# A Swin block on one core: the output projection as three float16 products of an output split on POOL, and a new order at the end of each step

## Chip, cores and metric

The kernel runs on 1 core of one Trainium2 chip. The metric is device time in microseconds (us) of one execution, and versions are compared by the median of several runs.

## What is computed

The input is x, 32 images of 96 channels by 56 by 56 pixels, float32. The reference is one Swin transformer block with shifted windows:

```python
f = roll(ln(x over channels) * g1 + b1, (-3, -3))
win = windows of 7 x 7 tokens                   # 64 windows per image
q, k, v = split(win @ w_qkv + b_qkv)            # 12 heads of 8
attn = softmax(q @ k.T * 8 ** -0.5 + mask)      # mask: shifted regions
out = (attn @ v) @ w_proj + b_proj              # the projection
f = x + roll(unwindow(out), (3, 3))
y = f + gelu(ln(f) @ w_fc1 + b_fc1) @ w_fc2 + b_fc2
```

## The kernel before

**Tiling.** An image is cut into 8 bands of 7 rows; one band is 8 windows, 392 tokens (TOK). There are 256 bands. The program is a software pipeline: one step per band, and in step t each stage works on band t plus a fixed offset. A band is loaded at offset LOAD = 9, reordered into windows on POOL at ORDER = 7, transposed to tokens at TURN = 6, normalised there and transposed back at BACK = 5, multiplied into queries and keys at QK = 4, into values at VALUES = 2; its scores are made and their maximum is taken at SCORE = 2; the shifted scores and their exponentials come at PROB = 0; the weighting with the values, its division, the transposes of the output and the projection at WEIGH = -1. The second layer norm of a finished band rides along with the first of a later one (8 bands apart, AFTER), then the hidden layer follows at offsets -5 and -4, its contraction at -6 and -5, the result at -7 and -6. Even and odd steps differ: the hidden layer of two bands (`expand`, `expand_rest`, Gelu) is done in odd steps, and its contraction (`contract`, L637) in even steps, so work repeats in pairs of steps.

**Order.** Each engine has its own program, written out by hand in a function `step(t)`; nothing reorders it. Engines meet through semaphores that count up. The orders that matter here:

- TensorE (L662). Odd step: three parts of shifted scores (L512), values (L473), scores (L494) and weighting (L530), then `turn` (L555), `expand`, `expand_rest`, `max_transpose` (L597), `out_transposes` (L608), `back` (L570), `queries_keys` (L438), `project` (L618). Even step: scores, weighting, shifted scores, values and so on, `turn`, `out_transposes`, `back`, `max_transpose`, `queries_keys`, `project`, `contract` (L652, L658). The first shifted scores of a step wait for n_low, the low half of the normalised tokens (xfl).
- ScalarE (L772). It takes the exponentials (L719), copies values (L713), writes the high float16 halves xfh (`back_high`, L731) and nat (`queries_keys_high`, L739), copies the transposed output to oT (`out_by_channel`, L753), copies the row of maxima (L745), and does the Gelu in odd steps (L762) and `scaled` in even ones (L770). The Gelu and the exponential each need a table load (ACT_TABLE_LOAD). In odd steps the Gelus come ahead of `out_by_channel`.
- VectorE (L923). The step begins with `residual` (L905) of the step before, which adds the projection in PSUM and the bias to x. In odd steps there follow `back_low` (xfl, L891) and `queries_keys_low` (L898) of the step before, `result` (L920, three additions of two SBUF tensors each) and `maxima` (L856) in turn, then `divide` (L863, L865), the last maxima, `by_token` (L872), `stats` (L880, L885), and `back_low` of this step.
- POOL (L414). Even steps begin with two `split_hidden` (L389 a copy to float16, L392 the subtraction that gives the low half). Every step then has `normalise` (L399, L402, L406, L411) and `order_x` (L378, L381, L382). `normalise` waits in L402 for n_made, that is for `back`; `back` of the next step waits for its result.
- SyncE issues all DMAs: images in and out, and nat by way of DRAM into the stacked operands kst, qbd, qst and kbd.

**Products.** Queries and keys, values, the hidden layer and its contraction are each computed as three float16 products of operands split into a high and a low half (high x high, high x low, low x high). The projection is one float32 product, with oT and wp. In the trace a float32 product has two records.

**Waits that matter.** `back` in an odd step waits for the first Gelu, because it writes the PSUM banks (B) that the Gelu reads:

```python
if odd(t):
    wait(pe, gelu_done, t.step(HIDDEN[0]).count(1, 1)) if has(t.step(HIDDEN[0])) else None
```

## Time and profile before

| what | value |
|---|---|
| median of 3 runs | 2875.02 us (2874.71 to 2877.26) |
| the profiled execution's own time | 2881.17 us |
| its span | 2879.4 us |
| TensorE busy (matmul) | 2719.4 us, 94% |
| VectorE busy | 2398.4 us, 83% |
| ScalarE busy | 2128.1 us, 74% |
| POOL busy | 1847.1 us, 64% |
| DMA | 358.88 MB, mean 125 GB/s |
| mean granted TensorE clock | 0.994 |

How to read it: the span is the time between the first and the last instruction of one profiled execution; durations in the rows below come from that execution. In the rows PE is the matmuls of TensorE and PEld its weight loads, DVE is VectorE, ACT is ScalarE, POOL is GpSimd. L12 is line 12 of the kernel. A matmul's duration reaches to the end of its pipeline, so that matmuls one behind the other overlap in the rows: the distance of two starts is what one costs.

### The profile page before, as it was taken

The numbers are of one execution on the slowest core, as the hardware profiler recorded it, in microseconds if no ns is written. First come the engines' busy times: TensorE is split into PE (matmuls) and PEld (weight loads), VectorE is DVE, ScalarE is ACT, GpSimd is POOL, SyncE is SP. The second block draws the span as 40 slices with busy tenths as digits, with TensorE's granted clock in tenths as the row PEclk, the third lists the DMA queues.
The fourth block names the chain that finished last, engine by engine and source line by source line (L and its number), as shares of the span: only waits on it lengthen the run. The fifth ranks groups of instructions, "written<-read, shape, count | busy, mean of one in ns | idle before, by whom it ended". The sixth has DMA issues, their size and how long they took to land.

```text
span 2879.4 us, 138054 instructions
## 1 busy us (share of the span) xinstructions
PE 2719.4 (94%) x55491; PEld 2243.8 (78%) x55491; DVE 2398.4 (83%) x6634; ACT 2128.1 (74%) x3464; POOL 1847.1 (64%) x2344
## 2 busy tenths in 40 slices
PE   4899999999999999999999999999999999999997
PEld 2787787878878878788788888788777877878875
DVE  7888888888888888888888888888888888888884
ACT  2677777777777777777777777777777777777774
POOL 3466666666666666666666666666666666666665
PEclk9999999999999999999999999999999999999998
DMA  2545545545545544454554554554545455455441
GB/s 73 135 123 132 130 125 129 131 127 131 130 127 132 129 126 127 128 134 126 129 132 124 130 134 124 130 131 125 129 124 131 125 131 133 123 130 134 123 117 29
DMA packets 414852, 358.88 MB, mean 125 GB/s; under 512 B 63646, under 2 KB 414176, under 8 KB 414204
## 3 DMA queue, kind: packets, MB, share of 16 engines
q1 hardware_dynamic: 414220, 350.04, 47.1%
q8 instruction: 447, 7.32, 1.1%
q14 instruction: 185, 1.52, 0.2%
HBM read 193.29 MB, written 154.14 MB: 121 GB/s over the span
## 4 chain that ended last, share of the span: by engine, by line
PE 77%; DVE 8%; ACT 8%; issue 6%; POOL 1%; SPq 0%; DMA 0%; POOLq 0%; DVEq 0%
PE psum L530 18%; PE psum L512 11%; PE psum L438 9%; PE psum L494 8%; PE psum L570 7%; PE psum L555 6%; PE psum L448 5%; DVE xfl L891 4%; ACT probs L719 4%; ACT xfh L731 4%; PE psum L608 3%; PE psum L618 3%; PE psum L456 3%; PE psum L473 2%; PE psum L597 1%
## 5 line engine op out<-in xcount | busy, mean ns | idle before, releaser
L719 ACT ACTIVATE probs<-psum 113x784 f32<-113x784 f32 x768 | 633.2, 824 | 348.6 <-PE psum L512 345.5
L856 DVE TENSOR_REDUCE nmax<-psum 113x16 f32<-113x784 f32 x768 | 743.4, 968 | 69.9 <-PE psum L494 69.8
L530 PE MATMUL psum<-vbd,probs 128*49 128x18 f32 x24576 | 643.8, 197 | 11.6 <-issue 11.4
L530 PEld LDWEIGHTS psum<-vbd,probs 128*49 128x49 f32 x24576 | 633.0, 126 | 15.2 <-issue 14.8
L399 POOL TENSOR_SCALAR ve<-mv 112x7 f32<-112x7 f32 (+1 forms) x264 | 65.9, 250 | 890.6 <-PE psum L570 649.6
L512 PE MATMUL psum<-qbd,kst 128*49 128x196 f16 x6144 | 404.9, 250 | 81.6 <-DVE xfl L891 70.7
L494 PE MATMUL psum<-kbd,qst 128*49 128x196 f16 x6144 | 403.1, 250 | 7.4 <-DVE nmax L856 4.9
L406 POOL TENSOR_TENSOR rs<-ve,half 112x7 f32<-112x7 f32 (+1 forms) x264 | 394.4, 1494 | 0.0
L411 POOL TENSOR_TENSOR xn<-xn,rs 112x672 f32<-112x672 f32 (+1 forms) x264 | 343.0, 1299 | 73.9 <-POOL rs L406 73.9
L891 DVE TENSOR_TENSOR xfl<-psum,xfh 96x784 f16<-96x784 f32 (+1 forms) x264 | 252.9, 958 | 160.7 <-ACT xfh L731 159.5
L880 DVE BATCH_NORM_STATS2 st<-tok 112x6 f32<-112x96 f32 x1824 | 318.3, 246 | 59.2 <-ACT tok L726 45.0
L392 POOL TENSOR_TENSOR hidl<-hid,hidh 128x588 f16<-128x588 f32 x256 | 334.1, 1305 | 46.2 <-POOL hidh L389 46.2
L512 PEld LDWEIGHTS psum<-qbd,kst 128*49 128x49 f16 x6144 | 243.9, 103 | 135.2 <-issue 95.8
L402 POOL TENSOR_TENSOR xn<-tok,mv 112x672 f32<-112x672 f32 (+1 forms) x264 | 343.4, 1301 | 0.5 <-POOL ve L399 0.5
L494 PEld LDWEIGHTS psum<-kbd,qst 128*49 128x49 f16 x6144 | 261.9, 103 | 93.0 <-issue 76.8
L739 ACT ACTIVATE nat<-psum 96x784 f16<-96x784 f32 x256 | 210.0, 820 | 127.8 <-PE psum L438 127.8
L713 ACT ACTIVATE vbd<-psum 49x384 f32<-49x384 f32 x512 | 261.0, 510 | 7.2 <-PE psum L473 1.0
L570 PE MATMUL psum<-ident,xn 112*96 112x112 f32 x1951 | 236.7, 263 | 25.3 <-POOL xn L411 24.2
L920 DVE TENSOR_TENSOR yr<-ys,xf 96x343 f32<-96x343 f32 (+2 forms) x768 | 243.0, 368 | 15.2 <-ACT ys L770 15.2
L898 DVE SCALAR_TENSOR_TENSOR nat<-psum,nat 96x784 f16<-96x784 f32 x256 | 245.8, 960 | 0.0
L731 ACT ACTIVATE xfh<-psum 96x784 f16<-96x784 f32 (+1 forms) x264 | 212.7, 806 | 27.2 <-PE psum L570 26.9
L570 PEld LDWEIGHTS psum<-ident,xn 112*96 112x96 f32 x1951 | 184.3, 127 | 52.2 <-POOL xn L411 25.3
(102 smaller groups left out, 6069.1 us busy)
## 6 DMA issues: line engine op xcount, KB each, us to landing
stack_pages<-nat SPq DMA_DIRECT2D x256, 294.0 KB, 3.0
kst<-stack_pages SPq DMA_DIRECT2D x256, 220.5 KB
qbd<-stack_pages SPq DMA_DIRECT2D x1024, 55.1 KB
stack_pages<-nat SPq DMA_DIRECT2D x256, 147.0 KB, 2.1
xr<-in_x_dram SPq DMA_DIRECT2D x224, 147.0 KB, 2.7
out_dram<-yr SPq DMA_DIRECT2D x224, 147.0 KB, 2.1
qst<-stack_pages SPq DMA_DIRECT2D x256, 73.5 KB
kbd<-stack_pages SPq DMA_DIRECT2D x1024, 18.4 KB
```

Of the source, the lines that this page charges most:

```text
L392: nc.gpsimd.tensor_tensor(hidl[:, n, :, :], hid[:, n, :, :], hidh[:, n, :, :], ALU.subtract).then_inc(hid_low, 1)
L402: nc.gpsimd.tensor_tensor(xn[:, n, 0:groups, :], tok[:, n, 0:groups, :], mv[:, n, 0:groups, 0:1].to_broadcast(wide_by_token), ALU.subtract ...
L406: nc.gpsimd.tensor_tensor(rs[:, n, 0:groups], ve[:, n, 0:groups], half[0:SPAN, 0:groups], ALU.pow).then_inc(root_done, 1)
L411: nc.gpsimd.tensor_tensor(xn[:, n, 0:groups, :], xn[:, n, 0:groups, :], rs[:, n, 0:groups].rearrange("t (g a) -> t g a", a=1).to_broadcast ...
L494: last = nc.tensor.matmul(psum[W1 * w:W1 * w + L, A + p // 2, p % 2 * CH:(p % 2 + 1) * CH], qst[:, masked_slot(b), u, toks], kbd[:, b.c % ...
L512: last = nc.tensor.matmul(wide_bank()[W1 * w:W1 * w + L, LEFT + p // 2 * 4 * SPAN + p % 2 * CH:LEFT + p // 2 * 4 * SPAN + (p % 2 + 1) * CH ...
L530: last = nc.tensor.matmul(dst[:, :, h, :], probs[:, b.c % 2, h // 4, p, h % 4 * L:(h % 4 + 1) * L], vbd[:, b.c % 4, p * NH + h, :, :], sta ...
L570: last = nc.tensor.transpose(wide_bank()[0:C, LEFT + at * SPAN:LEFT + (at + 1) * SPAN], xn[:, b.c % 2, g, :], ident[0:SPAN, 0:SPAN])
L719: nc.scalar.activation(probs[0:PR, b.c % 2, u, :, :].rearrange("j (g q) k -> j g (q k)", g=2), wide_bank()[0:PR, LEFT:LEFT + 8 * SPAN].rea ...
L731: nc.scalar.activation(parts_of(xfh, b), by_channel(b), ACT.Copy).then_inc(n_high, 1)
L856: nc.vector.tensor_reduce(dst, psum[0:PR, A:A + 2, 0:2 * CH].rearrange("i g (q h j) -> i g q h j", q=2, j=L), axis=AX.X, op=ALU.max, negat ...
L891: nc.vector.tensor_tensor(parts_of(xfl, b), by_channel(b), parts_of(xfh, b), ALU.subtract).then_inc(n_low, 1)
```

## The change

The projection becomes three float16 products like the others: weights split once into wph and wpl (`split_wp`, scaled by GAIN = 64), the output split in each step on POOL into oTh and oTl (`split_out`, new, ahead of `normalise` and behind `split_hidden`). The bias b_proj becomes a row of the weights against a row of ones in oTh, and `residual` scales by 1/GAIN in place of adding the bias. `out_by_channel` waits for the split of the band before. `project` waits for the split's low half. In odd steps `out_transposes` moves to behind `turn`, and `out_by_channel` to ahead of the Gelus. In even steps `project` moves behind `contract`, and `back_high` (xfh) comes ahead of `queries_keys_high` (nat). The diff (declarations shortened):

```diff
@@ -117,8 +117,8 @@
         wh, wl = sb("wh", [FULL, 3 * C], F16), sb("wl", [FULL, 3 * C], F16)
         w1h, w1l = sb("w1h", [FULL, HID], F16), sb("w1l", [FULL, HID], F16)
         wp, w2 = sb("wp", [FULL, C]), sb("w2", [FULL, 3, C])
-        vec = sb("vec", [C, 6])
-        G1, B1, BP, G2, B2, BF = range(6)
+        vec = sb("vec", [C, 5])
+        G1, B1, G2, B2, BF = range(5)
 
         xr = sb("xr", [C, 4, WS, SIDE])
         xf = sb("xf", [C, 8, 2, TOK])
@@ -137,7 +137,9 @@
         probs = sb("probs", [FULL, 2, QUADS, PAIRS, CH])
         rsum = sb("rsum", [PR, 2, 2 * NH])
         on = sb("on", [PR, 2, 2, C])
-        oT = sb("oT", [FULL, TOK])
+        oT = sb("oT", [C, TOK])
+        oTh, oTl = sb("oTh", [FULL, TOK], F16), sb("oTl", [FULL, TOK], F16)
+        wph, wpl = sb("wph", [FULL, C], F16), sb("wpl", [FULL, C], F16)
         hid = sb("hid", [FULL, 2, 3, PART])
         hidh, hidl = sb("hidh", [FULL, 2, 3, PART], F16), sb("hidl", [FULL, 2, 3, PART], F16)
         w2h, w2l = sb("w2h", [FULL, 3, C], F16), sb("w2l", [FULL, 3, C], F16)
@@ -180,7 +182,8 @@
         p_made, exp_done = sem("p_made"), sem("exp_done")
         pv_made, o_inverted, o_normed = sem("pv_made"), sem("o_inverted"), sem("o_normed")
         ot_made, o_in, proj_made, f_made = sem("ot_made"), sem("o_in"), sem("proj_made"), sem("f_made")
-        w2_split = sem("w2_split")
+        w2_split, wp_split = sem("w2_split"), sem("wp_split")
+        o_high, o_low = sem("o_high"), sem("o_low")
         hid_high, hid_low, w2_wide, y_scaled = sem("hid_high"), sem("hid_low"), sem("w2_wide"), sem("y_scaled")
         fc1_made, gelu_done, fc2_made, y_made = sem("fc1_made"), sem("gelu_done"), sem("fc2_made"), sem("y_made")
 
@@ -262,10 +265,11 @@
                 const(w2[REST * m:REST * (m + 1), 1 + m, :], wfc2[FULL:HID, :])
             const(brow[C:C + 1, :], bqkv.rearrange("(a c) -> a c", a=1))
             const(brow1[C:C + 1, :], bfc1.rearrange("(a c) -> a c", a=1))
-            for n, v in ((G1, g1), (B1, b1), (BP, bproj), (G2, g2), (B2, b2), (BF, bfc2)):
+            for n, v in ((G1, g1), (B1, b1), (G2, g2), (B2, b2), (BF, bfc2)):
                 column(n, v)
 
             sp.wait_ge(filled, 1)
+            const(wp[C:C + 1, :], bproj.rearrange("(a c) -> a c", a=1))
             sp.dma_start(xfh[C:C + 1, :, :, :].rearrange("a n k t -> a (n k) t"), rows_d[0, 4:5, 0:8, :]).then_inc(rows_one, 16)
 
             def key_mask_rows():
@@ -391,6 +395,16 @@
                 alone(pool)
                 nc.gpsimd.tensor_tensor(hidl[:, n, :, :], hid[:, n, :, :], hidh[:, n, :, :], ALU.subtract).then_inc(hid_low, 1)
 
+            def split_out(b):
+                pool.wait_ge(o_in, b.count(2, 2))
+                alone(pool)
+                wait(pool, proj_made, b.count(1))
+                alone(pool)
+                nc.gpsimd.tensor_copy(oTh[0:C, :], oT[:, :]).then_inc(o_high, 1)
+                pool.wait_ge(o_high, b.count(1, 1))
+                alone(pool)
+                nc.gpsimd.tensor_tensor(oTl[0:C, :], oT[:, :], oTh[0:C, :], ALU.subtract).then_inc(o_low, 1)
+
             def normalise(b):
                 n, groups = b.c % 2, spans(b)
                 wide_by_token = [SPAN, groups, C]
@@ -417,6 +431,8 @@
                     for offset in RESULT:
                         if has(t.step(offset)):
                             split_hidden(t.step(offset))
+                if has(t.step(WEIGH)):
+                    split_out(t.step(WEIGH))
                 if filling and has(t.step(ORDER)):
                     order_x(t.step(ORDER))
                 if turns(t.step(TURN)):
@@ -612,10 +628,14 @@
                 b = t.step(WEIGH)
                 if not has(b):
                     return
-                pe.wait_ge(o_in, b.count(2, 2))
+                pe.wait_ge(o_low, b.count(1, 1))
                 if has(t.step(SCORE)):
                     pe.wait_ge(max_row, t.step(SCORE).count(1, 1))
-                nc.tensor.matmul(psum[0:C, V_BANK, 0:TOK], wp[:, :], oT[:, :], start=True, stop=True).then_inc(proj_made, 1)
+                if first(b, 0):
+                    pe.wait_ge(wp_split, 3)
+                for n, (weights, rows) in enumerate(((wph, oTh), (wph, oTl), (wpl, oTh))):
+                    last = nc.tensor.matmul(psum[0:C, V_BANK, 0:TOK], weights[:, :], rows[:, :], start=n == 0, stop=n == 2)
+                last.then_inc(proj_made, 1)
 
             def expand(t, n):
                 b = t.step(HIDDEN[n])
@@ -671,12 +691,12 @@
                     shifted(t, 2)
                     scores(t, 2)
                     turn(t)
+                    out_transposes(t)
                     expand(t, 0)
                     expand(t, 1)
                     expand_rest(t, 0)
                     expand_rest(t, 1)
                     max_transpose(t)
-                    out_transposes(t)
                     back(t)
                     queries_keys(t)
                     project(t)
@@ -695,8 +715,8 @@
                     back(t)
                     max_transpose(t)
                     queries_keys(t)
+                    contract(t)
                     project(t)
-                    contract(t)
 
             steps(pe, step)
 
@@ -749,6 +769,7 @@
             def out_by_channel(t):
                 b = t.step(WEIGH)
                 act.wait_ge(ot_made, b.count(1, 1))
+                wait(act, o_low, b.count(1))
                 for d in range(2):
                     nc.scalar.activation(oT[0:C, d * 2 * PT:(d + 1) * 2 * PT].rearrange("c (p w t) -> c p w t", p=2, w=2),
                                          psum[0:C, O_BANK, d * 4 * W1:(d + 1) * 4 * W1].rearrange("c (w p t) -> c p w t", w=2, p=2)[:, :, :, 0:L],
@@ -779,9 +800,9 @@
                     run(VALUES, value_blocks)
                     run(PROB, exps, 1)
                     run(PROB, exps, 2)
+                    run(WEIGH, out_by_channel)
                     run(HIDDEN[0], gelu, 0)
                     run(HIDDEN[1], gelu, 1)
-                    run(WEIGH, out_by_channel)
                     run(SCORE, max_rows)
                     if turns(t.step(BACK)):
                         back_high(t)
@@ -794,9 +815,9 @@
                         by_token(t)
                     run(WEIGH, out_by_channel)
                     run(SCORE, max_rows)
-                    run(QK, queries_keys_high)
                     if turns(t.step(BACK)):
                         back_high(t)
+                    run(QK, queries_keys_high)
                     run(RESULT[0], scaled, 0)
                     run(RESULT[1], scaled, 1)
 
@@ -809,10 +830,11 @@
             nc.vector.memset(psum[:, :, :], 1.0).then_inc(psum_clear, 1)
             nc.vector.memset(w2[REST:FULL, 1, :], 0.0)
             nc.vector.memset(w2[0:REST, 2, :], 0.0)
-            for a in (wide, wide1, wp, xfh, xfl, oT):
+            for a in (wide, wide1, wp, xfh, xfl, oTh, oTl):
                 last = nc.vector.memset(a[FILL:FULL], 0.0)
             last.then_inc(filled, 1)
             dve.wait_ge(filled, 1)
+            nc.vector.memset(oTh[C:C + 1, :], 1.0)
             dve.wait_ge(consts_in, 16 * N_CONST)
 
             g = vec[:, G1:G1 + 1]
@@ -840,6 +862,13 @@
                 dve.wait_ge(w2_split, 1)
                 nc.vector.tensor_tensor(w2l[:, :, :], w2[:, :, :], w2h[:, :, :], ALU.subtract).then_inc(w2_wide, 1)
 
+            def split_wp():
+                nc.vector.tensor_scalar(wp[:, :], wp[:, :], GAIN, None, ALU.mult).then_inc(wp_split, 1)
+                dve.wait_ge(wp_split, 1)
+                nc.vector.tensor_copy(wph[:, :], wp[:, :]).then_inc(wp_split, 1)
+                dve.wait_ge(wp_split, 2)
+                nc.vector.tensor_tensor(wpl[:, :], wp[:, :], wph[:, :], ALU.subtract).then_inc(wp_split, 1)
+
             def key_zeros():
                 nc.vector.memset(kbd[:, :, :, :], 0.0)
                 nc.vector.memset(qst[:, :, :, :], 0.0).then_inc(keys_zero, 1)
@@ -902,8 +931,8 @@
                 b = t.step(WEIGH)
                 dve.wait_ge(proj_made, b.count(1, 1))
                 wait(dve, y_made, b.count(1, -7))
-                nc.vector.scalar_tensor_tensor(out=xf[:, b.c % 8, 1, :], in0=psum[0:C, V_BANK, 0:TOK], scalar=vec[:, BP:BP + 1], in1=xf[:, b.c % 8, 0, :],
-                                               op0=ALU.add, op1=ALU.add).then_inc(f_made, 1)
+                nc.vector.scalar_tensor_tensor(out=xf[:, b.c % 8, 1, :], in0=psum[0:C, V_BANK, 0:TOK], scalar=1 / GAIN, in1=xf[:, b.c % 8, 0, :],
+                                               op0=ALU.mult, op1=ALU.add).then_inc(f_made, 1)
 
             def result(t, n):
                 b = t.step(STORE[n])
@@ -952,6 +981,7 @@
                 if first(t, 1 - TURN):
                     stack_zeros()
                     split_w2()
+                    split_wp()
 
             steps(dve, step)
 
```

## Rows read from the trace of the kernel before

**Rows 1.** the page's first part: busy time, share of the span, instructions
```profile
PE 2719.4 (94%) x55491; PEld 2243.8 (78%) x55491; DVE 2398.4 (83%) x6634; ACT 2128.1 (74%) x3464; POOL 1847.1 (64%) x2344
```

**Rows 2.** the waits of the whole span: engine, line, releaser: us in total, times, longest
```profile
PE psum L512 <- DVE xfl L891: 70.7, 128, 2.2
...
ACT hid L762 <- PE psum L456: 84.5, 128, 2.3
```

**Rows 3.** the timeline of TensorE at an even step's end: start, duration, line
```profile
1413.47 0.33 PE L438 MATMUL psum<-xfh,wl 128*96 128x392 f16 x1
...
1413.63 0.82 PE L618 MATMUL psum<-oT,wp 128*96 128x392 f32 x2
...
1414.29 0.25 PE L652 MATMUL psum<-hidh,w2h 128*96 128x196 f16 x1
...
1415.86 0.25 PE L658 MATMUL psum<-hidh,w2l 64*96 64x196 f16 x2
...
1416.62 0.53 PE L512 MATMUL psum<-qbd,kst 128*49 128x196 f16 x8 [0.52 <-DVE xfl L891]
...
1419.24 0.53 PE L494 MATMUL psum<-kbd,qst 128*49 128x196 f16 x8
```

**Rows 4.** the timeline of VectorE over the same stretch
```profile
1414.49 0.62 DVE L905 SCALAR_TENSOR_TENSOR xf<-psum,vec,xf 96x392 f32<-96x392 f32 x1
...
1415.40 0.97 DVE L891 TENSOR_TENSOR xfl<-psum,xfh 96x784 f16<-96x784 f32 x1 [0.28 <-ACT xfh L731]
...
1417.17 0.69 DVE L920 TENSOR_TENSOR yr<-ys,xf 96x343 f32<-96x343 f32 x3
...
1418.04 0.98 DVE L856 TENSOR_REDUCE nmax<-psum 113x16 f32<-113x784 f32 x1 [0.18 <-PE psum L494]
```

**Rows 5.** the timeline of POOL over the same stretch
```profile
1411.81 0.67 POOL L389 CAST hidh<-hid 128x588 f16<-128x588 f32 x1
...
1412.66 1.30 POOL L392 TENSOR_TENSOR hidl<-hid,hidh 128x588 f16<-128x588 f32 x1 [0.18 <-POOL hidh L389]
...
1414.61 0.25 POOL L399 TENSOR_SCALAR ve<-mv 112x7 f32<-112x7 f32 x1 [0.65 <-DVE mv L885]
...
1417.89 1.31 POOL L411 TENSOR_TENSOR xn<-xn,rs 112x672 f32<-112x672 f32 x1 [0.27 <-POOL rs L406]
...
1419.14 0.78 POOL L378 COPY xf<-xr 96x343 f32<-96x343 f32 x1
```

**Rows 6.** groups of instructions by line and shape, POOL's L402: busy, mean ns, idle
```profile
L402 POOL TENSOR_TENSOR xn<-tok,mv 112x672 f32<-112x672 f32 x256 | 336.8, 1316 | 0.5 <-POOL ve L399 0.5
...
L402 POOL TENSOR_TENSOR xn<-tok,mv 112x384 f32<-112x384 f32 x8 | 6.6, 830 | 0.0
```

**Rows 7.** the timeline of TensorE at an odd step's end
```profile
1400.64 0.33 PE L448 MATMUL psum<-xfh,w1h 128*128 128x392 f16 x1
...
1402.66 0.55 PE L608 MATMUL psum<-ident,on 113*96 113x113 f32 x4
...
1403.17 0.94 PE L570 MATMUL psum<-ident,xn 112*96 112x112 f32 x8
```

**Rows 8.** the timeline of ScalarE in the odd and the even step
```profile
1400.51 1.28 ACT L762 ACT_TABLE_LOAD   x1
...
1402.40 1.21 ACT L762 ACTIVATE hid<-psum 128x588 f32<-128x588 f32 x2 [0.61 <-PE psum L456]
...
1412.27 0.54 ACT L753 ACTIVATE oT<-psum 96x196 f32<-96x196 f32 x2
```

**Rows 9.** single L920 from the timeline; L378's durations, ns, least/median/most
```profile
1417.17 0.50 DVE L920 TENSOR_TENSOR yr<-ys,xf 96x343 f32<-96x343 f32 x1
...
1418.94 0.63 DVE L920 TENSOR_TENSOR yr<-ys,xf 96x343 f32<-96x343 f32 x1
...
L378 POOL COPY xf<-xr x256: 490/498/792, 5.0 to 2766.4; 96x343 f32<-96x343 f32 x128
```

**Rows 10.** the stretch 60 to 80 us while the pipeline fills; granted clock third from last
```profile
60.00:80.00 20.00, 14.99 (x279) 12.04 (x278) 13.54 (x33) 10.17 (x17) 6.43 (x11) 0.89 0.48 126
```

## The prediction

> **What bounds the kernel now.** I began with the page: TensorE is busy 94% of the span, VectorE 83% [rows 1]. Work repeats in pairs of steps, about 22 us each, 128 in all, so I read one pair closely. The waits show few stops that recur in every pair: the pair's odd step starts with L512 waiting for xfl on VectorE, 70.7 us over 128 times, 0.55 each; and ScalarE waits 84.5 us over 128 times, 0.66 each, for the first hidden product before its Gelu [rows 2]. The timelines of one even step's end say what a shift of work meets. On TensorE the last queries-and-keys product starts at 1413.47, the float32 projection at 1413.63, the contraction runs from 1414.29 to about 1415.95 (its last products start at 1415.86), and then TensorE stands until L512 at 1416.62 [rows 3]. VectorE does the residual L905 at 1414.49, xfl at 1415.40 to 1416.37, and L512 follows 0.25 later [rows 3, 4]. So the path into the odd step is: projection, residual, xfl, L512. That order is fixed: VectorE's program has the residual ahead of back_low, and the diff leaves it so. Before, the projection was ready early enough that residual ended about 1415.11 and xfl waited only for ScalarE (0.28 idle in its row).
>
> **The change, part by part.** All times below are on the clock of this pair.
>
> *Three float16 products for one float32.* The float32 projection held TensorE 0.66 (1413.63 to 1414.29); a float16 product of 392 columns follows the one before by 0.16 (1413.47 to 1413.63), so three take 0.50 and the last result is out 0.16 later [rows 3]. Gain 0.16 a step, 0.32 a pair: this is all that the change can win on TensorE, 128 x 0.32 = 41 us.
>
> *The split on POOL.* No row has it; the nearest are L389 and L392, 588 columns at 0.67 and 1.30 with 0.18 between [rows 5]. L402 takes 1.316 at 672 columns and 0.830 at 384 [rows 6], so about 0.18 is fixed; scaled to 392 columns L389 gives 0.51 and L392 0.93. Bounds for the subtraction: 0.84 (L402 at 392) to 1.30 (no scaling). I take 0.93, the row of the same kind and types: 0.51 + 0.18 + 0.93 = 1.62.
>
> *Odd step: out transposes behind the turn.* The turn's successor starts at 1400.64; four transposes take 0.55 there as at 1402.66, so they are out at 1401.2 [rows 7]. ScalarE then copies oT (0.54 for two, as in the even step) ahead of the Gelu, to 1401.75. But the Gelu's table load of 1.28 started at 1400.51, under a wait; now it starts after the copies, and Gelu starts at 1403.05 instead of 1402.40: the 0.65 of idle that hid the load is used up [rows 2, 8]. back() of the odd step waits for that Gelu; its transposes started at 1403.17, right behind the Gelu's first half (1402.40 + 0.66), and now come at 1403.82 [rows 7, 8]. Less the 0.16 to 0.25 that the projection saves, the even step starts about 0.43 later. POOL's split here falls at 1401.85 to 1403.5, where POOL idles: nothing. But POOL's L402 of the odd step waits for back's n_made, so POOL's chain moves about 0.2. Bounds of this part: 0 (if the load were put ahead of the copies) to 0.65.
>
> *Even step: the split ahead of normalise, the projection behind the contraction.* POOL's second L392 started at 1412.66; its next instruction could start at 1413.91, so with the 0.2 the split runs 1414.1 to 1415.73 [rows 5]; its input is in by 1413.3, since oT's copies start at 1412.27 [rows 8]. TensorE, 0.43 late, ends queries and keys at 1414.06, and the contraction (1.66 long) at 1415.72 [rows 3]. Both arrive together. With 0.15 from signal to product, projection at 1415.9, result at 1416.56; residual (0.62, the next overlapping it by 0.08) from 1416.60; xfl 1417.13 to 1418.10; L512 at 1418.35 where it was at 1416.62 [rows 3, 4]: **+1.73**. Even with a free split and no odd shift the order alone does this: contraction ends at 1415.29, result at 1415.95, L512 at 1417.73, +1.1. xfh ahead of nat frees ScalarE's part early, but xfl stands behind the residual, so I cost it at nothing gained or lost: ScalarE's nat comes about when it did, and its save on SP's queue moves under 0.4 ahead of work that itself moves 1.7. SP gets no new transfer in the steps; the three small VectorE instructions and the constant's row are start-up, under 2 us.
>
> *A collision that follows.* VectorE comes to L920, the adds with two SBUF inputs, at 1417.17 before; 1.73 later is 1418.90. POOL's normalise starts behind the split, at 1415.73 instead of 1414.61, so its big multiply L411 moves from 1417.89 to 1419.01 [rows 4, 5]. Those two do not run together: the L920 issued at 1418.94 while L411 ran to 1419.20 took 0.63 instead of 0.50 and ended 0.37 after L411, and POOL's L378 beside it took 0.78 against 0.49 to 0.50 elsewhere [rows 4, 5, 9]. Today the first L920 trio falls in POOL's free time; in the new order it starts 0.1 ahead of L411, which takes over after its first add (about 1419.26) and holds the other two adds until 1420.57. The maximum L856 starts at about 1420.69 instead of 1418.04, and scores(1) on TensorE, which needs its end plus 0.05, start at 1421.72 instead of 1419.24 [rows 3, 4]. **Sum: +2.48 a pair**, 0.75 beyond the late residual. Behind it everything keeps its distances: the reciprocal waits for TensorE, statistics feed POOL, and POOL was idle there.
> The page SBUF — State Buffer of the Trainium skill, section on the port contention, says that a VectorE operation with two SBUF inputs and a GpSimd operation that reads SBUF lock each other out for the whole instruction. Taken to the letter, L411 would start at L920's end, 1419.40, and the pair would cost 2.62: 17 us more. The rows show the hand-over some 0.14 earlier, and I follow them.
>
> Pairs with all parts in them: 125. 125 x 2.48 = 310. The profiled execution took 2881.2 (span 2879.4), so 3191; the median of the runs is 6 lower, 2875.0, which makes **3185**.
>
> **The rivals.** (a) *Late residual, no collision*: L920 gets through before L411, or the loss is absorbed in the slack of 0.2 before scores(1). +1.73 a pair, 125 x 1.73 = 216: 3091. For it: the two instructions start only 0.1 apart. Against: the trio takes 0.69 and L411 1.31, so a shift of under half a microsecond doesn't part them [rows 4, 5]. (b) *Order alone*: the split is covered, the load stays hidden, +1.1: 125 x 1.1 = 138, 3013. Needs POOL to be done by 1415.3, 0.4 before my sum. (c) *Faster*: the late residual is absorbed because xfh comes earlier and L512 isn't held; then the 41 us of TensorE stay: 2834. It decides if xfl could end before the contraction does; for it speaks only that xfl waits for ScalarE today, against it VectorE's order of program and the 0.55 that L512 waits in each of 128 pairs. (d) *Equal*: gains and waits cancel, or the order has no effect because L512 is held elsewhere; nothing in the rows supports it. (e) *Worse*: the longer stand of TensorE, near 2 us in each pair, costs clock. While the pipeline fills, TensorE is busy 15 of 20 us and the granted clock is 0.89 [rows 10]: between the two levels, 2.4 and 1.2 GHz. TensorE's 21 us of work per pair at 0.89 would be 2.6 longer, 125 x 2.6 = 325 more: 3510. I expect 86% busy and no such fall.
>
> **How the numbers follow.** Full forecast 0.58, (a) 0.22, (b) 0.08, (c) 0.05, (d) 0.02, (e) 0.05. The forecast's own range: the odd shift from 0 to 0.65 and the split from 1.5 to 2.0 move it by -0.4 to +0.4 a pair, 3135 to 3235. To hold 8 in 10 it must reach over (a), 3050 at its low end; (b), (c), (d) and (e) are left out. A measurement of this kernel can tell about 0.2%, 6 us: faster 0.05, same 0.02, slower 0.93.
>
> **What would show it.** Right: L905 waits for L618's successor on TensorE about 2 us in every even step; L512's wait for xfl grows from 0.55 to near 1.8; the Gelu no longer waits for TensorE; one L920 of the first trio takes over 1.3 us; a pair lasts 24.4 us; TensorE busy near 86%. Wrong: L905 starting right behind the statistics, or a pair under 22 us. If the L920 rows look as before and L512 waits long, it is (a); if the projection starts at the contraction's end with POOL done long before, (b); if the granted clock falls, (e).

## The result and the profile after

The changed kernel takes 3186.35 us (median; 3183.75 to 3186.58) against 2875.3 us: ratio 1.108, interval 1.106 to 1.110. Its profiled execution has a span of 3182.0 us and a granted clock of 0.988. The lengths of a pair in the profiles, taken from each second residual to the next, have the median 24.06 us where it was 21.58: +2.48 a pair. The mean grew less, from 21.73 to 24.13, since more of the old pairs were longer than the common one.

The page, for [rows 1]:

```profile
PE 2694.7 (85%) x55747; PEld 2270.6 (71%) x55747; DVE 2483.1 (78%) x6639; ACT 2147.5 (67%) x3464; POOL 2200.2 (69%) x2856
```

TensorE has 25 us less to do and a share 9 points lower: the time is waiting. The waits of the whole span, for [rows 2] (engine, line, releaser: us in total, times, longest):

```profile
PE psum L528 <- DVE xfl L920: 222.3, 129, 1.9
DVE xf L934 <- PE psum L637: 214.4, 129, 3.2
...
PE psum L586 <- issue: 104.8, 127, 1.0
...
PE psum L510 <- DVE nmax L885: 85.1, 118, 1.1
...
ACT hid L783 <- PE psum L472: 4.6, 2, 2.9
```

(L528 was L512, L920 was L891, L934 was L905, L637 was L618, L510 was L494, L885 was L856, L949 was L920, L425 was L411, L586 was L570.) The first row of an odd step's shifted scores waits 1.7 where it waited 0.55; the residual, which hardly ever waited, waits 1.7; and the Gelu's wait for TensorE, which hid its table load, is gone (4.6 us in all where it was 84.5). Two waits are new in nearly every pair: `back` in the odd step stands 0.8, and scores wait for the maxima. One pair on TensorE, for [rows 3, 7]:

```profile
1599.45 0.53 PE L510 MATMUL psum<-kbd,qst 128*49 128x196 f16 x8
...
1607.40 0.25 PE L672 MATMUL psum<-hidh,w2h 128*96 128x196 f16 x1
...
1609.14 0.37 PE L637 MATMUL psum<-oTh,wph 128*96 128x392 f16 x1
...
1611.57 0.53 PE L528 MATMUL psum<-qbd,kst 128*49 128x196 f16 x8 [1.74 <-DVE xfl L920]
...
1615.21 0.53 PE L510 MATMUL psum<-kbd,qst 128*49 128x196 f16 x8 [0.83 <-DVE nmax L885]
```

VectorE over the same stretch, for [rows 4]:

```profile
1609.87 0.56 DVE L934 SCALAR_TENSOR_TENSOR xf<-psum,xf 96x392 f32<-96x392 f32 x1 [1.70 <-PE psum L637]
1610.36 0.96 DVE L920 TENSOR_TENSOR xfl<-psum,xfh 96x784 f16<-96x784 f32 x1
...
1612.12 2.15 DVE L949 TENSOR_TENSOR yr<-ys,xf 96x343 f32<-96x343 f32 x3
1614.19 0.96 DVE L885 TENSOR_REDUCE nmax<-psum 113x16 f32<-113x784 f32 x1
```

and POOL, for [rows 5]:

```profile
1608.05 0.92 POOL L406 TENSOR_TENSOR oTl<-oT,oTh 96x392 f16<-96x392 f32 x1 [0.18 <-POOL oTh L403]
1608.95 0.24 POOL L413 TENSOR_SCALAR ve<-mv 112x7 f32<-112x7 f32 x1
...
1612.21 1.58 POOL L425 TENSOR_TENSOR xn<-xn,rs 112x672 f32<-112x672 f32 x1 [0.27 <-POOL rs L420]
1613.74 0.49 POOL L382 COPY xf<-xr 96x343 f32<-96x343 f32 x1
```

Read them together: the projection comes behind the contraction, the residual behind it, xfl behind the residual, L528 behind xfl. Then the first trio of adds starts 0.09 before POOL's multiply L425 and takes 2.15 where it took 0.69; the multiply takes 1.58 where it took 1.31.

This pair is not quite the common one: it lasts 24.20, and POOL is 0.3 later in it. In 107 of the 118 pairs away from the ends of the span the multiply starts 0.19 ahead of the trio and keeps its 1.31; the trio's first add is then held for 1.48 and the trio takes 2.02. The pair before is of that kind, on VectorE and on POOL:

```profile
1588.05 2.02 DVE L949 TENSOR_TENSOR yr<-ys,xf 96x343 f32<-96x343 f32 x3
```

```profile
1587.86 1.31 POOL L425 TENSOR_TENSOR xn<-xn,rs 112x672 f32<-112x672 f32 x1 [0.27 <-POOL rs L420]
1589.11 0.78 POOL L382 COPY xf<-xr 96x343 f32<-96x343 f32 x1
```

### The profile page after: what moved, and what is told of

It reads as the page before. It is cut to its first block, busy times and chain, and to the rows that moved or that the text cites. A ratio compares the mean times of both kernels' runs of the same rounds, so it can differ in the third digit from the quotient of the medians.

```text
span 3182.0 us, 140105 instructions
## 1 busy us (share of the span) xinstructions
PE 2694.7 (85%) x55747; PEld 2270.6 (71%) x55747; DVE 2483.1 (78%) x6639; ACT 2147.5 (67%) x3464; POOL 2200.2 (69%) x2856
## 3 DMA queue, kind: packets, MB, share of 16 engines
q14 instruction: 197, 1.61, 0.2%
## 4 chain that ended last, share of the span: by engine, by line
PE 69%; DVE 18%; issue 8%; ACT 3%; POOL 1%; POOLq 0%; DMA 0%; DVEq 0%; ACTq 0%
PE psum L546 13%; PE psum L454 8%; PE psum L510 7%; PE psum L528 7%; PE psum L586 6%; PE psum L571 6%; DVE yr L949 5%; PE psum L637 5%; PE psum L672 4%; PE psum L464 4%; DVE xfl L920 4%; DVE nmax L885 4%; ACT probs L739 3%; DVE nat L927 3%; PE psum L624 3%
## 5 line engine op out<-in xcount | busy, mean ns | idle before, releaser
L885 DVE TENSOR_REDUCE nmax<-psum 113x16 f32<-113x784 f32 x768 | 743.1, 968 | 45.1 <-PE psum L510 43.3
L528 PE MATMUL psum<-qbd,kst 128*49 128x196 f16 x6144 | 403.4, 251 | 232.6 <-DVE xfl L920 222.3
L403 POOL CAST oTh<-oT 96x392 f16<-96x392 f32 x256 | 130.2, 509 | 662.7 <-ACT oT L774 662.5
L510 PE MATMUL psum<-kbd,qst 128*49 128x196 f16 x6144 | 403.5, 251 | 86.8 <-DVE nmax L885 85.1
L528 PEld LDWEIGHTS psum<-qbd,kst 128*49 128x49 f16 x6144 | 241.6, 103 | 305.1 <-issue 265.8
L920 DVE TENSOR_TENSOR xfl<-psum,xfh 96x784 f16<-96x784 f32 (+1 forms) x264 | 251.4, 952 | 197.3 <-ACT xfh L751 197.3
L425 POOL TENSOR_TENSOR xn<-xn,rs 112x672 f32<-112x672 f32 (+1 forms) x264 | 346.0, 1311 | 73.6 <-POOL rs L420 73.6
L510 PEld LDWEIGHTS psum<-kbd,qst 128*49 128x49 f16 x6144 | 259.5, 104 | 153.1 <-DVE nmax L885 112.4
L949 DVE TENSOR_TENSOR yr<-ys,xf 96x343 f32<-96x343 f32 (+2 forms) x768 | 343.2, 497 | 12.7 <-ACT ys L791 12.7
L586 PE MATMUL psum<-ident,xn 112*96 112x112 f32 x1951 | 236.0, 262 | 133.2 <-issue 104.8
L934 DVE SCALAR_TENSOR_TENSOR xf<-psum,xf 96x392 f32<-96x392 f32 x256 | 142.6, 557 | 214.4 <-PE psum L637 214.4
L586 PEld LDWEIGHTS psum<-ident,xn 112*96 112x96 f32 x1951 | 183.6, 127 | 159.8 <-issue 124.1
L406 POOL TENSOR_TENSOR oTl<-oT,oTh 96x392 f16<-96x392 f32 x256 | 236.4, 923 | 46.8 <-POOL oTh L403 46.8
```

The costliest lines, as they stand in the source:

```text
L425: nc.gpsimd.tensor_tensor(xn[:, n, 0:groups, :], xn[:, n, 0:groups, :], rs[:, n, 0:groups].rearrange("t (g a) -> t g a", a=1).to_broadcast ...
L510: last = nc.tensor.matmul(psum[W1 * w:W1 * w + L, A + p // 2, p % 2 * CH:(p % 2 + 1) * CH], qst[:, masked_slot(b), u, toks], kbd[:, b.c % ...
L528: last = nc.tensor.matmul(wide_bank()[W1 * w:W1 * w + L, LEFT + p // 2 * 4 * SPAN + p % 2 * CH:LEFT + p // 2 * 4 * SPAN + (p % 2 + 1) * CH ...
L586: last = nc.tensor.transpose(wide_bank()[0:C, LEFT + at * SPAN:LEFT + (at + 1) * SPAN], xn[:, b.c % 2, g, :], ident[0:SPAN, 0:SPAN])
L885: nc.vector.tensor_reduce(dst, psum[0:PR, A:A + 2, 0:2 * CH].rearrange("i g (q h j) -> i g q h j", q=2, j=L), axis=AX.X, op=ALU.max, negat ...
L920: nc.vector.tensor_tensor(parts_of(xfl, b), by_channel(b), parts_of(xfh, b), ALU.subtract).then_inc(n_low, 1)
```

## Experiments

Theory: the even step's residual is late, and this carries the adds into POOL's multiply. Rivals: POOL's split itself is what the projection waits for; the odd step's late Gelu is the loss; the lock costs nothing. Lengths of pairs and of trios below are medians from the profiles where nothing else is said; a row shows one pair, which can differ from them.

**order_alone**: one swap in the kernel before.

```diff
-                    project(t)
                     contract(t)
+                    project(t)
```

> The kernel before with one swap: in even steps contract comes ahead of project; float32 projection, no split. Theory (the order delays the residual, and the shift then runs L920 into POOL's L411): on the clock of the prediction's pair the contraction runs 1413.63 to 1415.37, the result is out at 1416.19, L512 starts 1.35 later than before, the first L920 trio comes at 1418.5 while L411 runs to 1419.20, and scores(1) start about 1.8 later. 125 pairs x 1.8 = 225: about 3100 us (3050 to 3140). Rival (POOL's split is what costs, the order is free): 2875 us.

Measured 3151.6 us, ratio 1.096 (1.094 to 1.098), above my range. The median pair is 23.42, that is +1.84, as worked out; but some 4 pairs in 10 last 1.2 longer. So the order costs nearly all of it with no split at all, and something else is on top. Windows of 1 us of such a pair show it (after the stretch: sum, five engines' busy time, granted clock, DMA share, GB/s):

```profile
1544.00:1545.00 1.00, 0.00 (x1) 0.00 (x0) 0.96 (x2) 0.27 (x1) 1.00 (x1) 1.00 0.51 152
...
1546.00:1547.00 1.00, 1.00 (x23) 1.00 (x21) 1.00 (x2) 0.31 (x1) 1.00 (x2) 0.50 0.31 68
1547.00:1548.00 1.00, 1.00 (x24) 1.00 (x21) 0.84 (x3) 0.86 (x2) 0.95 (x3) 0.50 0.02 6
1548.00:1549.00 1.00, 1.00 (x28) 1.00 (x26) 0.70 (x1) 0.68 (x2) 0.00 (x0) 0.50 0.21 56
```

Behind the 1.80 in which TensorE stands before L512, the granted clock is 0.50, the 1.2 GHz level, in the rows from 1546 to 1549, and what TensorE does there takes nearly twice as long: from L512 to the next scores it is 1.57 (1545.80 to 1547.37), and 0.86 in the kernel before. The lock is there without a split too; in another pair:

```profile
1522.98 1.49 DVE L920 TENSOR_TENSOR yr<-ys,xf 96x343 f32<-96x343 f32 x3
```

**order_filler**: order_alone with work for that stand.

```diff
                     project(t)
+                    if has(t.step(WEIGH)) and has(t.step(PROB)):
+                        for _ in range(12):
+                            nc.tensor.matmul(psum[0:C, O_BANK, 0:3 * C], wh[:, 0:C], wl[:, :], start=True, stop=True)
```

> order_alone with 12 more float16 products of 288 columns at the end of each even step, into the free out bank, results unused: about 1.4 us more work for TensorE a pair, in the 1.8 us in which it stands before L512. Theory (the extra 50 us of order_alone over its 23.4 us pair come from TensorE's clock falling to its lower level after that stand in 4 pairs of 10): the clock stays up, L512 starts as late as before, no pair of 24.6 is left. Mean pair 23.4 to 23.5: 3095 us (3080 to 3115), although work was added. Rival (the long pairs have another cause, or the stand is not idle on the path): 3152 us or more.

Measured 3091.4 us, ratio 1.074 (1.072 to 1.076); median pair 23.37, mean 23.41, longest 23.73; clock 0.994 against 0.967. L512 starts as late as in order_alone (12.38 behind the even step's first scores in both). More work, 60 us less time: the long pairs were the clock.

```profile
1516.07 1.63 PE L702 MATMUL psum<-wl,wh 128*96 128x288 f16 x12
1518.03 0.53 PE L512 MATMUL psum<-qbd,kst 128*49 128x196 f16 x8 [0.33 <-DVE xfl L894]
```

**xfl_first**: VectorE's order in the changed kernel.

```diff
-                run(before, WEIGH, residual)
                 if odd(t):
                     if turns(before.step(BACK)):
                         back_low(before)
+                    run(before, WEIGH, residual)
...
                 else:
+                    run(before, WEIGH, residual)
```

> The changed kernel, with VectorE's back_low (xfl) of the step before ahead of the residual in odd steps. Theory: xfl then runs at 1608.2 (on the clock of the changed kernel's pair that starts its odd step at 1611.57), L512 follows TensorE's own work at about 1609.8, 1.8 earlier, and the first L920 trio ends before L411 starts at 1612.2; the second trio now meets L411, which costs back 0.7 to 0.9, and values wait 0.4 for the residual. A pair goes from 24.06 to about 22.1 us: 3186 - 125 x 1.96 = 2940 us (2890 to 2990). Rival (the late residual is not what holds L512, but POOL or the odd step is): 3186 us.

Measured 2971.3 us, ratio 1.033 (1.031 to 1.035); pair 22.29. L528 starts 0.26 behind the last product of the projection, its wait for xfl is 1.1 us in the whole span, and VectorE shows the lock gone from the first trio (0.69) and come to the second, which takes 1.24 in most pairs and 1.52 in this one:

```profile
1503.47 0.94 DVE L920 TENSOR_TENSOR xfl<-psum,xfh 96x784 f16<-96x784 f32 x1
1505.25 0.56 DVE L934 SCALAR_TENSOR_TENSOR xf<-psum,xf 96x392 f32<-96x392 f32 x1 [0.84 <-PE psum L637]
...
1506.61 0.69 DVE L949 TENSOR_TENSOR yr<-ys,xf 96x343 f32<-96x343 f32 x3
...
1508.25 1.52 DVE L949 TENSOR_TENSOR yr<-ys,xf 96x343 f32<-96x343 f32 x3
```

One order on one engine gives back 215 of the 311 us. Of the 0.71 a pair that is left over the kernel before, 0.45 stands between the odd step's turn and the even step's first scores, where the late Gelu is.

**maxima_first**: the changed kernel, the first maxima ahead of the first trio.

```diff
-                    run(t, STORE[0], result, 0)
                     run(t, SCORE, maxima, 0)
+                    run(t, STORE[0], result, 0)
                     run(t, STORE[1], result, 1)
```

> The changed kernel, with the step's first maxima (L885) ahead of the first L920 trio on VectorE in odd steps; the residual stays late. Theory (collision of L920 and L425 on the way to scores(1)): scores(1) start up to 1.0 earlier; since the two trios then stand between the first and second maxima, 0.3 to 0.4 comes back. 125 x 0.65 = 81: about 3105 us (3060 to 3120). Rival (no collision cost, the whole 2.49 a pair is the late residual and the odd step): 3186 us or a little more.

Measured 3123.7 us, ratio 1.086 (1.085 to 1.088), pair 23.35: 0.71 less, where 0.65 was worked out. The time is 19 us over my number and just outside the range, as some pairs last up to 24.9. Neither trio meets the multiply now, so that the stretch from L528 to scores(1) is 2.62 as in the kernel before and not 3.51: the lock cost 0.89 there. 0.17 comes back behind it, where both trios now stand. The late residual is untouched (12.11 to L528, as in the changed kernel).

**project_first**: the changed kernel with the swap of order_alone undone.

```diff
-                    contract(t)
                     project(t)
+                    contract(t)
```

> The changed kernel, with project put back ahead of contract in even steps. Theory: the split on POOL ends within 0.1 to 0.2 us of the contraction, so the projection waits for POOL instead and gives its result at the same time; the contraction then fills TensorE while VectorE works. Pair 24.0 to 24.1: 3186 us within 20. Rival (the contraction ahead of the projection is the whole cause, POOL's split is hidden): a pair 1.1 or more shorter, 3050 us or less.

Measured 3155.0 us, ratio 1.097 (1.096 to 1.099), pair 23.82: neither. The projection now waits for POOL:

```profile
1519.35 0.37 PE L637 MATMUL psum<-oTh,wph 128*96 128x392 f16 x1 [1.17 <-POOL oTl L406]
```

and starts 9.27 after its even step's first scores (1510.08) where it started 9.69 after them (1609.14 less 1599.45). So POOL is ready 0.4 before the contraction's end, not 0 to 0.2. The adds now start 0.18 ahead of the multiply, and the trio takes 2.16: that takes back 0.16 of the 0.41 won. Contraction and split hold the projection back by nearly the same, so that taking either away alone gives little; no run takes both away.

**short_low**: POOL's subtraction for 8 columns.

```diff
-                nc.gpsimd.tensor_tensor(oTl[0:C, :], oT[:, :], oTh[0:C, :], ALU.subtract).then_inc(o_low, 1)
+                nc.gpsimd.tensor_tensor(oTl[0:C, 0:8], oT[:, 0:8], oTh[0:C, 0:8], ALU.subtract).then_inc(o_low, 1)
...
+            nc.vector.memset(oTl[0:FILL], 0.0)
```

> The changed kernel with POOL's subtraction (the low half of the output) done for 8 of 392 columns only, the rest of the low half left zero: that part of the projection is left out; about 0.7 us less POOL work a step. Theory (the projection waits for the contraction, not for POOL; the split's length acts through the lock): L512 stays 12.1 after the even step's start; L425 moves 0.7 ahead, to end about 0.7 after the first L949 is issued; the first maxima start 0.5 to 0.6 earlier. A pair 23.5: about 3117 us (3090 to 3140). Rival 1 (the projection waits for the split): L512 itself comes 0.4 or more earlier and the pair goes below 23.3. Rival 2 (POOL has no part in it): 3186 us.

Measured 3152.6 us, ratio 1.096 (1.094 to 1.098), pair 23.80. L528 stays where it was, 12.13 after the even step's start (1521.41 less 1509.28; 12.12 in the changed kernel): the projection does not wait for the split. The trio (L950 in this kernel's lines) takes 1.75 instead of 2.02 (the medians; 1.73 in the row), so the split's length acts through the lock. The gain is 0.26 a pair and not 0.55: normalise had to wait 0.41 for VectorE's statistics, which I had left out, and POOL's next copy still met the trio, which starts 0.47 behind L425, where it was 0.19, and not 0.7.

```profile
1521.96 1.73 DVE L950 TENSOR_TENSOR yr<-ys,xf 96x343 f32<-96x343 f32 x3
```

```profile
1518.19 0.25 POOL L413 TENSOR_SCALAR ve<-mv 112x7 f32<-112x7 f32 x1 [0.41 <-DVE mv L915]
```

**odd_undone**: the changed kernel with the odd step's order as before, on TensorE and on ScalarE.

```diff
                     turn(t)
-                    out_transposes(t)
...
                     max_transpose(t)
+                    out_transposes(t)
...
-                    run(WEIGH, out_by_channel)
                     run(HIDDEN[0], gelu, 0)
                     run(HIDDEN[1], gelu, 1)
+                    run(WEIGH, out_by_channel)
```

> The changed kernel with the odd step's order put back: out_transposes behind max_transpose, out_by_channel behind the Gelus. Theory (the odd move costs 0.3 a pair by the late Gelu but pays by letting POOL split while it idles): the split then starts only when oT is in, about 1.6 later after the turn than in the changed kernel, normalise and the hidden splits behind it come 1.3 to 1.6 later, and the even step's projection waits for POOL. A pair grows from 24.06 to about 25.3: 3346 us (3290 to 3380). Rival (the late Gelu is a main part of the loss): a pair 0.3 shorter, 3150 us.

Measured 3371.5 us, ratio 1.172 (1.170 to 1.173), pair 25.45. Undoing the odd move costs 1.4 a pair: what POOL no longer does in its idle time outweighs what the late Gelu costs, and the projection now waits for POOL in both steps, 0.89 in the odd one below and 0.21 in the even one behind it. The way from the turn to the even step's first scores became 6.72, longer than the 6.21 of the changed kernel, so that this run does not show the late Gelu's cost by itself; and from those scores to L528 it takes 12.86 instead of 12.11.

```profile
1510.43 0.37 PE L637 MATMUL psum<-oTh,wph 128*96 128x392 f16 x1 [0.89 <-POOL oTl L406]
```

**xfh_ahead, xfh_xfl_ahead, three_moves**: the kernel before, with float32 projection. The first takes only the change's swap on ScalarE (xfh ahead of nat in even steps), the second adds VectorE's order of xfl_first, the third moves the second trio:

```diff
-                    run(QK, queries_keys_high)
                     if turns(t.step(BACK)):
                         back_high(t)
+                    run(QK, queries_keys_high)
```

```diff
-                    run(t, STORE[1], result, 1)
                     run(t, SCORE, maxima, 1)
...
                     stats(t)
+                if odd(t):
+                    run(t, STORE[1], result, 1)
                 if odd(t) and turns(t.step(BACK)):
                     back_low(t)
```

> The kernel before with back_high (xfh) ahead of queries_keys_high (nat) in even steps, nothing else. Theory (xfl waited 0.28 a pair for ScalarE, and L512 for xfl): xfl starts behind the residual, 0.28 earlier, and L512 with it; part comes back, since the second L920 trio still waits for L411's end at 1419.20. 0.1 to 0.28 a pair: about 2855 us (2835 to 2868). Rival (this order doesn't matter, as I costed it in the changed kernel): 2875 us.

> The kernel before with xfh ahead of nat in even steps, and VectorE's back_low of the step before ahead of the residual in odd steps. Theory (chain residual, xfl, L512): L512 now follows the contraction, 0.6 earlier; the second L920 trio waits longer for L411 and the second maxima gate about half of it away. 0.3 a pair: 2837 us (2800 to 2860). Rival (L512's 0.55 wait for xfl is off the path that sets the period): 2875 us.

> As xfh_xfl_ahead, and the second L920 trio (result(1)) moved behind stats at the odd step's end, where VectorE waits 0.77 for xfh and POOL only starts normalise. Theory (lock between L920 and L411 is what gave the gain back): the full 0.55 to 0.6 a pair stays, 21.0 a pair: 2803 us (2780 to 2830). Rival (the lock costs nothing there, or the later store of y holds up SP's queue): no better than xfh_xfl_ahead.

Measured 2864.9 (ratio 0.995, 0.994 to 0.997), 2860.4 (0.994, 0.992 to 0.995) and 2818.2 us (0.979, 0.977 to 0.980). The first two gain less than worked out, and their median pair is 21.57 as before: all that L512 gained, 0.37 and 0.59 a pair, was lost again in one place, the second trio, which takes 1.55 and 1.76 where it took 1.18, since L411, which started 1.04 ahead of it, now starts 0.67 and 0.46 ahead. What they gain, 0.5% and 0.6%, is that fewer pairs are longer than the common one (means 21.64 and 21.61, from 21.73). A pair of xfh_xfl_ahead in which the second trio is held for longest, on VectorE and on POOL:

```profile
1516.06 2.05 DVE L920 TENSOR_TENSOR yr<-ys,xf 96x343 f32<-96x343 f32 x3
```

```profile
1515.89 1.31 POOL L411 TENSOR_TENSOR xn<-xn,rs 112x672 f32<-112x672 f32 x1 [0.27 <-POOL rs L406]
```

So POOL's L411 holds the second maxima at one time, however early L512 comes. With that trio moved the commonest pair is 20.97, the 0.6 that was forecast for the full gain; but the mean is 21.27, with pairs of up to 22.9, so the time is 15 us over my number, inside the range. three_moves beats the kernel before by 2.1% and has 88% of the changed kernel's time.

**after_two_moves**: the changed kernel with xfl_first's order and the second trio moved.

> The changed kernel with xfl ahead of the residual, and result(1) behind stats at the odd step's end: the late residual and the lock are both out of the way. Theory: beside xfl_first (pair 22.3) the second L920 trio no longer waits for L425, and scores(2) come 0.2 earlier: 22.0 to 22.1 a pair, 2940 us (2920 to 2965). What stays over the kernel before is the wait of values for the late residual (0.3), the contraction ahead of xfl's followers and the odd step's late Gelu (0.3). Rival (the split is worth its 0.32 a pair once the waits are gone): below 2875 us.

Measured 2990.8 us, ratio 1.039 (1.037 to 1.041), worse than xfl_first. The short pairs, nearly half of all, are 22.15, near what was worked out, but a third last 23.0 or more, up to 25.2 (mean 22.68, in xfl_first 22.46). More of TensorE's idle time there is ended by nothing that the profile shows; in after_two_moves and in xfl_first:

```profile
PE psum L546 <- issue: 31.6, 36, 1.7
```

```profile
PE psum L546 <- issue: 8.6, 18, 1.1
```

Those 23 us more are part of the 51 by which my number missed; the cause of the long pairs stays open. The rival falls in any case: with both waits gone the split doesn't earn its 0.32 a pair. three_moves has the same order on VectorE and the float32 projection; its common pair is 1.18 shorter, and 0.42 of this lies between the turn and the even step's first scores.

## Why the prediction was right

The forecast was 3185 us, and 3186.35 was measured. Both stretches that it named cost what it said within 0.15 a pair, and the experiments part them: xfl_first takes the late residual away, maxima_first the collision. The terms are set here against medians over 118 pairs of each profile, with the pair cut at four starts on TensorE: the odd step's first shifted scores, scores(1), the turn, and the even step's first scores.

- *Late residual.* From the even step's first scores to the odd step's first shifted scores it was 10.93 (1405.69, in the row below, to 1416.62 [rows 3]) and is 12.12 (1599.45 to 1611.57): +1.19. The prediction had +1.73 less the odd step's 0.43, so +1.30; 0.10 too much was the 0.15 from POOL's signal to the product, for which nothing waits. xfl_first shows that it is VectorE's order that turns this into time; order_alone, that no split is needed for it. The row of the kernel before, on TensorE:

```profile
1405.69 0.53 PE L494 MATMUL psum<-kbd,qst 128*49 128x196 f16 x8
```

- *Collision.* +0.75 was predicted. From L528 to scores(1) it takes 3.51 where it took 2.62: +0.89. In the pair shown above start, length and end of POOL's multiply came out as worked out (0.64 behind L528, 1.58, 2.22; worked out were 0.66, 1.56, 2.22), but it is one of 11 such pairs. In the other 107 POOL is earlier: the multiply leads by 0.19, and it is the first add and not the last two that stands. The sum left out that the adds are locked out once more, by POOL's next copy L382: in the common pair the second add takes 0.48 instead of 0.18, in the pair shown the third 0.51 instead of 0.17, and the first maxima start 2.49 and 2.62 behind L528, not 2.34.
- *Odd step.* +0.43 was predicted. From the turn to the even step's first scores it takes 6.21 where it took 5.76: +0.45. The transposes of `back` come 0.61 later behind the turn (3.84, 1621.28 less 1617.44, where the kernel before took 3.23, 1403.17 [rows 7] less 1399.94), and the projection saves 0.16 of it. No run takes the late Gelu away by itself. The short stretch from scores(1) to the turn, which the sum left as it was, takes 2.23 where it took 2.28.
- *POOL's split.* 1.62 was predicted; the cast takes 0.510, the subtraction 0.923, with 0.18 between, 1.61. But it doesn't arrive together with the contraction: it is ready 9.22 behind the even step's first scores, the projection starts at 9.68, and the prediction had 9.61 and 9.78. POOL's chain was said to move 0.2 with `back`; from the turn to the end of the odd step's multiply it takes 8.94 where it took 8.91, and the pair that the prediction read was one with 9.07. The nearest rival (b) was wrong all the same, since the order costs more than it was charged there: L920 meets L411 without a split too.
- *Sum.* 1.19, 0.89, 0.45 and -0.05 make the measured 2.48, where 1.30, 0.75 and 0.43 made 2.48: 0.11 too much in one term, 0.14 too little in another, and the closeness of the total is luck of that size. It is luck as well that 125 x 2.48 fits: by the means the pairs grew by 2.40, which is 300 us, and the profiled executions differ by 303 us, the medians of the runs by 311. The sign "a pair lasts 24.4" was counted from "about 22 us"; the common pair was 21.58 and is 24.06.
- *xfh ahead of nat* was costed at nothing and is nothing in the changed kernel by the rows, where xfl starts right behind the residual. In the kernel before xfl did wait for ScalarE [rows 4], and L512 comes 0.37 earlier with this swap; the common pair stays as it was, and the 0.5% won are fewer long pairs.
- *Clock.* The fall of rival (e) was expected not to come. It comes in few pairs of the changed kernel (mean clock 0.988) and in 4 of 10 of order_alone, with nearly the same stand, 1.74 and 1.80. In the changed kernel 9 of the pairs last 24.7 to 24.9, and they stand 314 to 362 us apart; in one of them, behind L528's wait of 1.74, the granted clock is 0.50, the 1.2 GHz level, in the row from 1516 to 1518. Why so much more in one kernel than in the other was not found out.

```profile
1516.00:1518.00 2.00, 2.00 (x48) 2.00 (x44) 2.00 (x3) 1.11 (x3) 1.47 (x4) 0.50 0.04 9
```

The section "Who interferes with whom" of the Trainium skill's SBUF — State Buffer held in its direction: 2.15 for the trio. By its letter, L425 would have started at the first add's end; it ended at 1613.79 (1612.21 + 1.58), which is 1.17 after that end (1612.12 + 0.50) for an instruction of 1.31. So the hand-over came 0.14 before the end, as the prediction took it from the rows. In the pair before, where the multiply was first, the first add ended 0.37 behind the multiply's end (1588.05 + 1.48, and 1587.86 + 1.31) and takes 0.50 by itself: 0.13 before the end as well.

## What to carry to other kernels

Before a product is moved behind other work to give its operand time, follow its result: here the first instruction of the next step on another engine consumed it, and everything behind that stood in line. When a change moves a stretch of one engine against another, look for pairs of VectorE and POOL operations that read SBUF and never overlapped before; in this kernel such a pair held up 0.89 of every 24 us, and parting it in maxima_first won 0.71 net, more than the 0.32 that the cheaper products save. And where a gain at one wait leaves the period as it was, as 0.37 and 0.59 did here, look for the place that takes it back, and move both. Read more than one pair: the one read closely here was one of 11 in 118 in its order of the two instructions.

## What the runs showed of the hardware

- TensorE's granted clock fell to the 1.2 GHz level behind stands of 1.80 us in 4 of 10 pairs of a loop of 23.4 us (mean clock 0.967), and did not when 1.63 us of unused products filled the stand (0.994): 60 us of 3152 were won by adding work.
- Two VectorE additions of 28 and 21 columns, which take 0.18 and 0.17, lasted 1.29 and 0.51 beside POOL's multiply (1.31 alone) and the copy behind it (0.49): the length of what holds them up counted, not their own. The first of them, on VectorE in the changed kernel:

```profile
1612.54 1.29 DVE L949 TENSOR_TENSOR yr<-ys,xf 96x28 f32<-96x28 f32 x1
```
